# Local attention's row maxima: pairs of heads stacked on the partitions, in chunks of 64 queries by 128 keys

## What is computed

```python
C = 64
kc = two_chunks(k)                # previous chunk and own chunk: 128 keys
scores = jnp.einsum('bhnid,bhnjd->bhnij', qc, kc) * scale
band = (j >= i) & (j <= i + C)
kv_global = (jnp.arange(nc)[:, None, None] - 1) * C + j[None]
mask = band[None] & (kv_global >= 0)
scores = jnp.where(mask[None, None], scores, jnp.finfo(scores.dtype).min)
probs = jax.nn.softmax(scores, axis=-1)
out = jnp.einsum('bhnij,bhnjd->bhnid', probs, vc)
```

## Time and profile before

| | us |
|---|---|
| median of 3 runs | 648.11 |
| lowest, highest | 645.52, 650.67 |
| the profiled execution | 643.76 |
| its span in the profile | 642.0 |
| TensorE busy (matmuls) | 597.1 |
| VectorE busy | 376.8 |
| ScalarE busy | 302.9 |
| POOL busy | 118.4 |

### The profile page before, as it was taken

The page is one execution under the profiler, slowest core; times in us unless marked ns, Lnnn a source line. Parts: engine busy times, 40 slices in busy tenths (PEclk is TensorE's granted clock), DMA queues, the critical chain, the costliest instruction groups (busy, mean ns, idle before and its releaser), DMA issues.

```text
span 642.0 us, 10723 instructions
## 1 busy us (share of the span) xinstructions
PE 597.1 (93%) x3890; PEld 466.9 (73%) x3890; DVE 376.8 (59%) x757; ACT 302.9 (47%) x466; POOL 118.4 (18%) x90
## 2 busy tenths in 40 slices
PE   4899999998999999999998897789999999999995
PEld 3788645687888888888886575553447778888885
DVE  7577757754435454454557799794376533344556
ACT  3667675463333333333333572458764643333331
POOL 4500031223111222222210000002201231222220
PEclk9998999999999999999999799899999999999999
DMA  8464674000111111111100034302310000111101
GB/s 316 126 225 135 221 213 136 2 26 19 31 26 49 49 49 49 49 49 32 44 23 1 0 93 125 118 18 88 90 39 1 26 25 26 50 49 50 49 1 65
DMA packets 22195, 44.66 MB, mean 70 GB/s; under 512 B 3632, under 2 KB 7632, under 8 KB 22160
## 3 DMA queue, kind: packets, MB, share of 16 engines
q1 hardware_dynamic: 21840, 44.05, 21.8%
q10 hardware_dynamic: 320, 0.13, 0.1%
HBM read 33.16 MB, written 11.01 MB: 69 GB/s over the span
## 4 chain that ended last, share of the span: by engine, by line
PE 70%; DVE 18%; ACT 5%; issue 3%; DMA 2%; POOL 1%; DVEq 0%; SPq 0%; ACTq 0%
PE PS L553 32%; PE PS L995 15%; DVE nmx L1581 5%; PE PS L878 4%; PE PS L847 2%; PE PS L714 2%; PE PS L712 2%; PE PS L826 2%; PE PS L831 2%; DVE stats L1479 1%; PE PS L725 1%; DVE x L1650 1%; PE PS L893 1%; DVE xn L1795 1%; DMA qk_slot<-rows_scr 1%
## 5 line engine op out<-in xcount | busy, mean ns | idle before, releaser
L1318 ACT ACTIVATE qk_hi<-xn 128x512 fp32r<-128x512 f32 x82 | 51.8, 631 | 166.8 <-DVE xn L1795 137.2
L553 PE MATMUL PS<-h_hi,wqkv_hi 128*128 128x512 f32 x304 | 103.0, 396 | 2.9 <-DVE h_lo L1513 2.2
L553 PE MATMUL PS<-h_hi,wqkv_lo 128*128 128x512 f32 x272 | 92.4, 396 | 1.8 <-DVE xn L1705 1.8
L1792 DVE TENSOR_TENSOR prs<-prs,PS 128x512 f32<-128x512 f32 x60 | 41.2, 687 | 84.6 <-PE PS L553 83.3
L519 POOL TENSOR_TENSOR wqkv_hi<-fw_raw,wqkv_hi 128x768 fp32r<-128x768 f32 x18 | 33.1, 1841 | 254.0 <-ACT wqkv_hi L1294 254.0
L1799 DVE TENSOR_TENSOR qk_lo<-xn,qk_hi 128x512 fp32r<-128x512 f32 x70 | 48.5, 692 | 50.4 <-ACT qk_hi L1318 50.4
L1314 ACT ACTIVATE prs<-PS 128x512 f32<-128x512 f32 x82 | 48.7, 594 | 49.5 <-PE PS L553 49.5
L553 PEld LDWEIGHTS PS<-h_hi,wqkv_hi 128*128 128x128 f32 x304 | 57.2, 188 | 15.3 <-DVE h_lo L1513 3.0
L553 PE MATMUL PS<-h_lo,wqkv_hi 128*128 128x512 f32 x160 | 62.9, 393 | 0.0
L553 PEld LDWEIGHTS PS<-h_hi,wqkv_lo 128*128 128x128 f32 x272 | 51.1, 188 | 13.3 <-DVE xn L1705 2.7
L1581 DVE TENSOR_REDUCE nmx<-PS 128x512 f32 (+4 forms) x96 | 54.2, 638 | 5.4 <-PE PS L730 5.2
(11 more groups left out here) (259 smaller groups left out, 1199.7 us busy)
## 6 DMA issues: line engine op xcount, KB each, us to landing
fw_raw<-in_ffn SPq DMA_DIRECT2D x41, 384.0 KB, 3.1
qk_slot<-rows_scr SPq DMA_DIRECT2D x32, 200.0 KB
rows_scr<-qk_hi SPq DMA_DIRECT2D x16, 256.0 KB
qk_slot<-q_scr SPq DMA_DIRECT2D x32, 100.0 KB
rows_scr<-qk_lo SPq DMA_DIRECT2D x8, 256.0 KB
wmod<-in_wmod SPq DMA_DIRECT2D x1, 1536.0 KB, 13.7
x<-in_x SPq DMA_DIRECT2D x2, 512.0 KB, 4.4
wmod<-in_wmod SPq DMA_DIRECT2D x1, 1024.0 KB, 10.1
```

Of the source, the lines that this page charges most:

```text
L553: ins = nc.tensor.matmul(dst, left(a, c), right(b, c), start=n == 0, stop=n == total - 1)
L1318: nc.scalar.activation(hidR[b][0], hid[b], ACT.Copy).then_inc(f["hi"], 1)
L1792: tt(hid[buf] if half is None else gu[buf], gact[buf], PS[:, 5, :], ALU.mult).then_inc(f["gu"], 1)
```

## The change

Two heads are taken together, as a pair: 64 queries of one and 64 queries of the other are stacked on the 128 partitions. A product then is one chunk of both heads' queries against the 128 keys that this chunk sees (64 keys for the first chunk). A bank holds 4 chunks of 128 columns, a pair is 8 chunks in two banks.

- The mask of a bank is one matmul of 512 columns. The table of masks has 128 columns for the first chunk and 128 for the later ones; `mask0[1]` repeats the latter by a stride of 0.
- TensorE's `scores` returns at even heads (after the wait for that head's `qm`), and forms the pair at odd heads. The work that stands between units keeps its place.
- ScalarE still masks one head a copy, into every other run of 64 columns of a pair's buffer. It waits until the whole pair two before is through.
- VectorE's `maxima` returns at even heads; at odd heads it reduces two banks of 512 columns to four columns of `nmx` each.
- The transposed maxima have the two heads side by side in the columns, so each part is stored by two transfers with runs of 64 elements, and the counts waited for are doubled.
- POOL makes the masks with four copies.

```diff
+        mask0 = [maskB[:, 0:MASKS0].rearrange("p (c k) -> p c k", k=P),
+                 maskB[:, P:2 * P].unsqueeze(1).to_broadcast([P, 4, P])]
...
+        qm0 = q_masked[:, :].rearrange("p (n c h q) -> p n c h q", n=2, h=2, q=WIN)
...
-                eng.dma_start(q_scr[l][b * H:(b + 1) * H, MAXROW[l] + part, :].rearrange("u (t q) -> u t q", q=P),
-                              mxT[part][:, b, :].bitcast(F32)).then_inc(at[l][f"mw{b}"], 16)
+                to = q_scr[l][b * H:(b + 1) * H, MAXROW[l] + part, :]
+                if l == 0:
+                    for h in range(2):
+                        eng.dma_start(to.rearrange("(n h) (c q) -> h n c q", h=2, q=WIN)[h],
+                                      mxT[part][:, b, h * WIN:(h + 1) * WIN].bitcast(F32)).then_inc(at[0][f"mw{b}"], 16)
...
-                        sp.wait_ge(at[0]["mw0"], 16 * 2)
+                        sp.wait_ge(at[0]["mw0"], 16 * 4)
...
+            nc.gpsimd.tensor_copy(maskB[:, 0:2 * P], mask_raw[:, 0:2 * P]).then_inc(consts, 1)
+            for to, n, raw in ((2 * P, P, mask_raw[:, P:2 * P]), (MASKS0, KEYS0, mask_raw[:, 2 * P:2 * P + KEYS0])):
...
-                    k = qkR[0][:, bass.ds(2 + (g - BQ * b) // 2, 1), :].rearrange("p m t -> p (m t)")
-                    for t in range(NT):
-                        bank, col = 2 * (s % 2) + t // 2, (t % 2) * KEYS0
-                        if t % 2 == 0:
-                            ge(a["mxd"], 2 * (u - 2) + t // 2 + 1)
-
-                            nc.tensor.matmul(PS[:, bank, 0:2 * KEYS0], identB[:, :], mask0[t // 2], start=True, stop=True)
-                        before = WIN * (t > 0)
-                        ins = nc.tensor.matmul(PS[:, bank, col + WIN - before:col + KEYS0], qm[s][:, t * P:(t + 1) * P],
-                                               k[:, t * P - before:(t + 1) * P], start=False, stop=True,
+                    if s % 2 == 0:
+                        return
+                    n = 2 * g + s // 2
+                    k = qkR[0][:, 2 + (g - BQ * b) // 2, :]
+                    for c in range(S // WIN):
+                        bank, col = 2 * (s // 2) + c // 4, (c % 4) * P
+                        if c % 4 == 0:
+                            ge(a["mxd"], 2 * (n - 2) + c // 4 + 1)
+                            nc.tensor.matmul(PS[:, bank, :].rearrange("p (c k) -> p c k", k=P), identB[:, :], mask0[c // 4],
+                                             start=True, stop=True)
+                        before = WIN * (c > 0)
+                        ins = nc.tensor.matmul(PS[:, bank, col + WIN - before:col + P],
+                                               qm0[:, s // 2, c, :, :].rearrange("p h q -> p (h q)"),
+                                               k[:, c * WIN - before:(c + 1) * WIN], start=False, stop=True,
                                                skip_group_check=True)
...
-                pe.wait_ge(at[0]["mxd"], 2 * (UNITS - 1))
+                pe.wait_ge(at[0]["mxd"], 2 * (PAIRS - 1))
...
-                ge(a["s"], (2, 3)[l] * (u - 3))
+                ge(a["s"], 3 * (u - 3) if l else 2 * (2 * g + s // 2 - 1))
...
+                if l == 0:
+                    of, to = of.rearrange("p (c q) -> p c q", q=WIN), qm0[:, s // 2, :, s % 2, :]
+                nc.scalar.activation(to, of, ACT.Copy, scale=headmask[:, bass.ds(4 * head + s, 1)]).then_inc(a["qm"], 1)
...
+                    if s % 2 == 0:
+                        return
+                    n = 2 * g + s // 2
                     for i in range(2):
-                        ge(a["s"], 2 * u + i + 1)
-                        nc.vector.tensor_reduce(nmx[:, bass.ds(NT * u + 2 * i, 2)],
-                                                PS[:, 2 * h + i, 0:2 * KEYS0].rearrange("p (t k) -> p t k", k=KEYS0),
+                        ge(a["s"], 2 * n + i + 1)
+                        nc.vector.tensor_reduce(nmx[:, bass.ds(2 * NT * n + NT * i, NT)],
+                                                PS[:, 2 * (s // 2) + i, :].rearrange("p (c k) -> p c k", k=P),
                                                 X, ALU.max, negate=True).then_inc(a["mxd"], 1)
...
+    chunk = np.arange(P)[None, :]
+    band = (chunk >= q % WIN) & (chunk <= q % WIN + WIN)
```

More of the change, by code:

```diff
@@ L70 @@
 EU = 2 * EARLY
-CONSTS = 19
+CONSTS = 20
+MASKS0 = 4 * P
 RSQRT_MAGIC = float(0x5F3759DF)
@@ L303, in store_maxima @@
                 eng.wait_ge(at[l][done], b + 1)
-                eng.dma_start(q_scr[l][b * H:(b + 1) * H, MAXROW[l] + part, :].rearrange("u (t q) -> u t q", q=P),
-                              mxT[part][:, b, :].bitcast(F32)).then_inc(at[l][f"mw{b}"], 16)
+                to = q_scr[l][b * H:(b + 1) * H, MAXROW[l] + part, :]
[3 more added lines that the diff above has]
+                                      mxT[part][:, b, h * WIN:(h + 1) * WIN].bitcast(F32)).then_inc(at[0][f"mw{b}"], 16)
+                else:
+                    eng.dma_start(to.rearrange("u (t q) -> u t q", q=P), mxT[part][:, b, :].bitcast(F32))\
+                        .then_inc(at[l][f"mw{b}"], 16)
         @block.sync
@@ L464, in _ @@
             pool.wait_ge(loaded["mask"], 16)
-            for to, (start, end) in ((0, (0, 2)), (2, (1, 3)), (4, (2, 5))):
-                nc.gpsimd.tensor_copy(maskB[:, to * KEYS0:(to + end - start) * KEYS0],
-                                      mask_raw[:, start * KEYS0:end * KEYS0]).then_inc(consts, 1)
+            nc.gpsimd.tensor_copy(maskB[:, 0:2 * P], mask_raw[:, 0:2 * P]).then_inc(consts, 1)
+            for to, n, raw in ((2 * P, P, mask_raw[:, P:2 * P]), (MASKS0, KEYS0, mask_raw[:, 2 * P:2 * P + KEYS0])):
+                nc.gpsimd.tensor_copy(maskB[:, to:to + 2 * n].rearrange("p (r n) -> p r n", n=n),
+                                      raw.unsqueeze(1).to_broadcast([P, 2, n])).then_inc(consts, 1)
+            nc.gpsimd.tensor_copy(maskB[:, MASKS0 + 2 * KEYS0:], mask_raw[:, 2 * P + KEYS0:]).then_inc(consts, 1)
             pool.wait_ge(loaded["csel"], 16)
@@ L1162, in mask_q @@
                 u = 4 * g + s
[L1163 removed]
+                ge(a["s"], 3 * (u - 3) if l else 2 * (2 * g + s // 2 - 1))
                 head = g - BQ * b
                 rows = (q1R[b] if l else qkR)[0]
[L1166 to L1167 removed]
+                of = rows[:, bass.ds(head // 2, 1), :].rearrange("p m t -> p (m t)").bitcast(F32)
+                to = qm[s][:, :]
+                if l == 0:
+                    of, to = of.rearrange("p (c q) -> p c q", q=WIN), qm0[:, s // 2, :, s % 2, :]
+                nc.scalar.activation(to, of, ACT.Copy, scale=headmask[:, bass.ds(4 * head + s, 1)]).then_inc(a["qm"], 1)
             def mask_first(l, b):
@@ L1898, in shape_tables @@
     c = np.arange(KEYS0)[None, :]
-    band = (c >= q) & (c <= q + WIN)
+    chunk = np.arange(P)[None, :]
+    band = (chunk >= q % WIN) & (chunk <= q % WIN + WIN)
     later = np.where(band, 0.0, NEG)
-    first = np.where(band & (c >= WIN), 0.0, NEG)
+    first = np.where(band & (chunk >= WIN), 0.0, NEG)
     causal = np.where(np.arange(P)[None, :] < q, 0.0, NEG)
```

21 lines of the change are left out of this document (9 added, 12 removed).

## The result

| | before | after |
|---|---|---|
| median, us | 646.92 | 656.32 |
| all executions, us | 650.67, 645.52, 648.11, 645.74 | 657.12, 657.3, 647.71, 655.52 |
| the profiled execution (span), us | 643.76 (642.0) | 657.12 (655.3) |
| TensorE's mean granted clock in it | 0.989 | 0.965 |

The ratio is 1.0127, interval 1.0077 to 1.0178. The forecast was 647.8 us, range 643.8 to 651.2, with 0.90 on no change. The median is 8.5 us above the forecast.

The account below looks back on a forecast made before the run. It took SyncE's train of stores and loads, ending at 81.54 us, as the bound, not TensorE or VectorE. Only 0.3 us reached the end: execution 643.76 to 643.5, median 648.11 to 647.8; range 643.8 to 651.2.

Parts of the forecast that it names:

- step 8: Behind 81.59 us, after the wait for slots: same work in the same order, so only 0.3 us reaches the end.
- the rivals of -2.7 and +1.4: Saved work arrives, 645.4 us, chance 0.20; small stores hold the loads, 649.5 us, chance 0.20 shared with a clock dip.
- the 8.5 us: Distance of the measured median, 656.32 us, above the forecast of 647.8 us.
- Prices: Engines' work after the change: TensorE 1.28 us a pair, VectorE 0.61 a reduction, ScalarE 0.655 a copy, POOL 0.
- the rival of 0.19 a product: TensorE's products stand farther apart, a pair costing 1.96 us in the maxima stage: slower, 654.3 us, chance 0.06.
- Steps 1, 2 and 4: TensorE in layer 0's maxima: third pair at 38.68 us, first sequence's end 48.21 (-0.36), second sequence's next score 59.62 (-0.15).
- Step 3: Second sequence's start on TensorE: clock dip left as it is, maxima transposed at 57.4 us instead of 58.2, -0.80.
- a second dip of the clock: In TensorE's pauses at 37 and 58 us, grown by 0.65: 1.0 us lost, chance 0.20 together with small stores.
- Steps 5 and 6: Low maxima end at 59.3 us; SyncE's train of stores and loads starts at about 60.5 instead of 60.58; 0.3 gained.
- Step 7: End of stage: keys-major products from 70.0 us; two more ScalarE issues cost 1.2, 0.7 reaching TensorE; loads land at 81.2.
- The saved work: Rival: the stage's end, 1.5 us earlier, and sooner-gone older stores reach the end: 2.7 us, 645.4, chance 0.20.
- Small stores hold the loads: Rival: 256-byte runs land 4 us after issue, delaying the eight loads: 649.5 us, chance 0.20 together with a clock dip.

Follow-up runs that it names:

- e1: The kernel before, unedited, measured as if it were the changed one: 649.82 us, ratio 1.0043.
- e9: The kernel before, unedited, again measured as its own rival in another group: 647.94 us, ratio 1.0020.
- e2: The changed kernel once more, unedited: 648.98 us, ratio 1.0052.
- e16: The changed kernel, unedited, run to count executions with a low clock: 648.01 us, ratio 1.0038.
- e3: The changed kernel with eight zero matmuls in layer 1's first keys-major steps: 649.86 us, ratio 1.0075.
- e6: The changed kernel with the second sequence's four stores of maxima issued by POOL instead of ScalarE: 646.92 us, ratio 0.9987.
- e10: The changed kernel, unedited, in another group: 649.38 us, ratio 1.0063.
- e11: The changed kernel with the second sequence's stores of maxima on POOL's queue, run again: 644.96 us, ratio 0.9991.
- e7: The kernel before with only layer 0's maxima stored in two transfers of 256-byte runs: 654.97 us, median of five executions, no ratio.
- e15: The changed kernel with POOL's queue for the stores and fillers in layer 0's waits and layer 1's first keys-major steps: 645.43 us, ratio 0.9997.
- e12: The changed kernel with POOL's queue, eight repeated masks and layer 1's fillers, but none in layer 0's wait for slots: 649.66 us, ratio 1.0049.
- e5: The changed kernel with eight repeated masks and eight zero matmuls in two of layer 0's TensorE waits: 646.00 us, ratio 0.9997.
- e8: The changed kernel with fillers in two of layer 0's TensorE waits and stores on POOL's queue: 654.67 us, five executions.

## Why the prediction was wrong, and where right

**What made the 8.5 us.** Most of it is no term of the sum: three of the first four executions had a mean clock of 0.964 or 0.965, the profiled one through a long stretch at half clock, a draw that both kernels make in one of six or seven executions and that costs some 10 us (low executions of before have a median of 656.7 us, the others 646.1). In the profiled execution it lay in layer 1, and with the late start of full clock it makes 12.8 of 13.3 us. The step that failed is step 8, "Behind 81.59 the same work stands in the same order. The 0.3 is all that reaches the end": the same work took 11.3 us more in layer 1's pass, at half clock. The range fell with it, "with that and the rivals of -2.7 and +1.4 the range is 643.8 to 651.2": it was built on the spread of three executions, 645.5 to 650.7, too few to show a draw of one in seven.

**How near it was otherwise is in part luck.** The forecast of 647.8 stands beside 648.0 in the executions after that are not low. But it started from 648.11, the median of three, 2 us above what the kernel before has without its low ones. Of the change itself it said -0.3 us. The executions that are not low say +1.9 against all of the kernel before (648.0 - 646.1) and -0.3 against e1 and e9 (648.35), so its sign is not settled. By its steps:

- *Prices.* TensorE 1.23 us a pair (forecast 1.28), VectorE 0.62 a reduction (0.61), ScalarE 0.64 a copy (0.655), POOL nothing on the path. Products of 128 columns come to (0.615 - 0.22)/4 = 0.10 each, under the 0.12 taken; the rival of 0.19 a product is refuted.
- *Steps 1, 2 and 4* came out within 0.2 us: 38.64 for 38.68, the first sequence's end at 49.46 - 1.43 = 48.03 for 48.21, 59.61 for 59.62. Masks that come late cost nothing more in the six pairs, 9.4 us for 9.53.
- *Step 3* took the dip of the clock as it is; it stayed (half clock from 52.5 for 3.4 us, 51.0 before), and the maxima are transposed at 58.73 - 1.43 = 57.30 for 57.4. But a second one came behind step 4, at 62.7, after a wait that had grown to 2.04 us. The prediction had named this among the rivals, "a second dip of the clock, in pauses that grow by 0.65 us at 37 and at 58", with 1.0 us. At 3.4 us with half the speed it costs 1.7, and the keys-major products begin at 73.06 - 1.43 = 71.63 instead of the 70.0 forecast; e2 and e16 don't have it there, the first profile, e3, e6, e10 and e11 do.
- *Steps 5 and 6*: the low part ends at 58.99 for 59.3, the train starts at 60.36 for 60.5, the loads at 62.42 for 62.4. Right.
- *Step 7* has the term that was sized wrong in the stage. It said: "two issues more, 1.2, of which 0.7 reaches TensorE. It comes to the waiting place at 79.6 instead of 80.4 and finds the loads landing at 81.2". The four issues took 3.1 us, not 2.5, and the exponential behind them came 1.9 us later than before (79.97 - 1.43 = 78.54, before 76.63). It reached TensorE as the wait of 1.91: from its first keys-major product to the waiting place TensorE took 10.6 us, before 8.9, so 1.75 us arrive where the forecast had 0.7. The ninth unit, which was to wait 1.6 to 2.3 us for its slots, started at 83.68 - 1.43 = 82.25 with no wait, 0.66 later than before. The wait for the train had turned into one for ScalarE. e7 and e6 show it from both sides: the extra issues alone bring it, and without them the ninth unit waits for its slots until 81.08, near the 81.2 forecast.
- *Step 8*, the same work in the same order behind, holds for instructions, not for the clock: besides the 27.3 us above, e2 and e16 have 6.8 and 13.7 us at half clock behind the wait for ScalarE, and the kernel before has 10.2 behind its wait for the slots in e1 and e9.

**The rivals.** The saved work did not arrive: in every profile of the kernel after the stage behind is held by ScalarE, in e6 and e11 by the train. Small stores hold the loads by their landing: refuted (2.3 and 1.8 us in e7; the changed kernel's own landings are not in its profile, but its eight loads go 0.26 us after SyncE's last issue ahead of them). What they cost is their issue on ScalarE. The Trainium skill, "DMA: Bandwidth & Descriptors", section Specifications, which wants 512 bytes for full rate, is neither confirmed nor refuted in that; at 16 KB a transfer the landing did not show it.

**Is there anything left of the 3.5 us?** A fit of time against the mean granted clock, over 37 and 140 executions and 23 of e6 and e11, gives 526 us for a clock of 1.0 more or less, and at equal clock the kernel after is 0.95 us (standard error 0.3) faster than before, that with POOL's queue 2.2 us (0.4). Fitted as a kernel of their own, e1 and e9 come out 0.6 us (0.4) slower than the program that they equal, so of these only the 2.2 is clearly larger than such a difference. The clock takes it back: in the executions that are not low its mean is 0.981 after and 0.987 before (0.985 in e1 and e9), and 0.0055 of 526 is 2.9 us. This is an estimate from a straight line, not a run. What was measured is that POOL's queue alone (e6, e11) and with all fillers (e15) ends at 0.9987 to 0.9997 of before, and with some (e12) at 1.0049: no version is clearly faster than the kernel before.

**What stays open.** Why in layer 1 the clock falls for 27 us in one execution and not in the next, in the same code. Five of the 18 profiles (after, e1, e5, e8, e9) have a stretch there, for 27.3 us in one and 3.4 in four. Whether fillers end it is not shown by 24 executions. Whether the change makes the kernel faster or slower is open as well, within some 2 us.

## What to carry to other kernels

Before the time of a kernel is compared, look at the granted clock of every execution: where some of them have a stretch at half clock in code that both versions share, four executions say little, and a control with equal programs tells what a ratio is worth; the control must be read as strictly as the change, or a difference that it shows too is put down to the change. Compare two traces at more than one point: what the changed kernel had lost at the ninth unit the kernel before lost behind it. Work saved on an engine ahead of a wait makes the wait longer, and here TensorE's waits of 1.35 to 2.06 us were mostly followed by stretches at half clock, in both kernels. Count the issues that a change adds to an engine's own queue at their full price, and move them to an idle one.

## What was not expected of the hardware

- TensorE can be busy for 100% of a stretch and stay at 1.2 GHz for it: 27.3 us in layer 1 (after) and 30.7 in layer 0 (e12), both in a pass whose products use 50 of the 128 rows or 17 or 32 of the 128 columns, both ended within the pass.
- Full clock is granted first at 15.8 to 17.5 us in some executions and at 21.3 to 23.9 in others of the same kernel (before: 16.8, e1: 23.9), and the first masking copy comes at 23.7 to 25.4 in the first and at 25.8 to 27.6 in the others. The Trainium skill, "TensorE: Matmul & The Clock Gate", section "Part 1: The HAM clock gate", says that the number of slow matmuls at the start differs from run to run of one kernel; the traces agree, with these numbers.
- A few executions have a mean clock of 0.56 to 0.84 and take 676 to 939 us: three of 143 of the kernel before and two of eleven of e5. None was profiled.
